# Windowed-attention block of a transformer kernel: shifted input and rotary tables made in earlier stages, query norms applied as the scale of the exponential, one wait moved

## The reference, cut to what matters

```python
h = shift_token(x)                    # channels 64..127 come from the token before
q, k, v = split(h @ wqkv)             # 8 heads of 64
q = l2norm(q) * qs;  k = l2norm(k) * ksc
q, k = rotary_xpos(q, k)              # q*cos*scale + rotate_half(q)*sin*scale, k with 1/scale
o = local_attention(q*8, k, v)        # windows of 64 tokens, 128 keys each, masked softmax
x = x + o @ wo
h = layernorm(shift_token(x)) * lg + lb
a, g = split(h @ w1 + b1);  x = x + (a * gelu(g)) @ w2 + b2
```

## Time and profile before

| | us |
|---|---|
| median of 3 runs | 1410.14 |
| the 3 runs | 1409.4 to 1416.5 |
| the profiled execution | 1428.19 |
| its span (first to last instruction) | 1426.4 |
| PE busy | 1167.5 (82%) |
| DVE busy | 915.8 (64%) |
| ACT busy | 588.9 (41%) |
| POOL busy | 420.4 (29%) |

### The profile page before, as it was taken

The page is one execution under the profiler, slowest core; times in us unless marked ns, Lnnn a source line. Parts: engine busy times, 40 slices in busy tenths (PEclk is TensorE's granted clock), DMA queues, the critical chain, the costliest instruction groups (busy, mean ns, idle before and its releaser), DMA issues. The chain is left out here.

```text
span 1426.4 us, 28851 instructions
## 1 busy us (share of the span) xinstructions
PE 1167.5 (82%) x11197; PEld 708.9 (50%) x11197; DVE 915.8 (64%) x1538; ACT 588.9 (41%) x1379; POOL 420.4 (29%) x357
## 2 busy tenths in 40 slices
PE   7899887899797768897867989556996799963997
PEld 5477644687544347652436754323662354422343
DVE  3677544777346867534885724487465689979387
ACT  2555434555333549533557822200562255420100
POOL 0366301566003875300884500433341000000000
PEclk9899999899987989999997999889997899975699
DMA  2000000000021210011220001000000011110011
GB/s 58 15 1 2 1 12 17 1 1 1 9 71 41 56 34 3 2 61 24 57 50 2 3 6 66 12 3 4 4 5 12 12 20 19 19 34 0 8 29 44
DMA packets 55146, 29.29 MB, mean 21 GB/s; under 512 B 37634, under 2 KB 48620, under 8 KB 54508
## 3 DMA queue, kind: packets, MB, share of 16 engines
q1 hardware_dynamic: 55020, 27.52, 7.8%
HBM read 18.32 MB, written 1.06 MB: 14 GB/s over the span
## 5 line engine op out<-in xcount | busy, mean ns | idle before, releaser
L287 POOL TENSOR_TENSOR A_pr<-A_pr,A_rs 128x1024 f32<-128x1024 f32 x64 | 121.1, 1893 | 78.4 <-DVE A_rs L350 76.1
L340 DVE TENSOR_REDUCE A_mx<-psb 128x1 f32<-128x1024 f32 x64 | 77.8, 1216 | 15.2 <-PE psb L300 14.8
L1058 POOL TENSOR_TENSOR F_raw<-F_raw,F_rc 128x1024 f32<-128x1024 f32 x32 | 75.3, 2354 | 39.8 <-DVE F_raw L1133 39.8
L1077 PE MATMUL psb<-F_wqkv,F_hst 128*128 128x512 f32 x128 | 66.0, 640 | 16.6 <-ACT F_hst L1149 16.6
L383 ACT ACTIVATE A_pr<-psb,A_nm 128x1024 f32<-128x1024 f32 x64 | 71.2, 1112 | 20.1 <-DVE A_nm L344 20.1
L321 PE MATMUL psb<-A_pt,A_V 128*64 128x128 f32 x1024 | 63.0, 275 | 13.8 <-issue 8.9
L1943 PE MATMUL psb<-M_hb,M_wd 128*128 128x512 f32 x128 | 73.3, 657 | 0.0
L1088 PE MATMUL psb<-ident,F_raw 128*128 128x128 f32 x256 | 38.5, 298 | 42.2 <-POOL F_raw L1061 42.2
L1750 ACT ACTIVATE M_hall<-psb,M_bu 128x512 f32<-128x512 f32 x64 | 44.0, 687 | 64.8 <-PE psb L1701 64.8
L310 PE MATMUL psb<-ident,A_pr 128*128 128x128 f32 x512 | 68.8, 278 | 1.4 <-ACT A_pt L390 1.4
L1701 PE MATMUL psb<-XL,M_wu 128*128 128x512 f32 x128 | 68.7, 619 | 1.5 <-ACT M_ST L1761 1.1
(11 more groups left out here) (331 smaller groups left out, 2979.4 us busy)
## 6 DMA issues: line engine op xcount, KB each, us to landing
F_VS<-F_V SPq DMA_DIRECT2D x62, 128.0 KB, 2.3
F_raw<-in_c_xpos_dram SPq DMA_DIRECT2D x3, 1024.0 KB, 4.8
F_wqkv<-in_L_ffn_wqkv_dram SPq DMA_DIRECT2D x3, 768.0 KB, 6.2
A_w<-in_L_attn_w_dram SPq DMA_DIRECT2D x4, 256.0 KB, 3.0
M_wu<-in_L_ffn_Wup_dram SPq DMA_DIRECT2D x16, 64.0 KB, 2.0
M_wg<-in_L_ffn_Wgate_dram SPq DMA_DIRECT2D x16, 64.0 KB, 2.1
M_wd<-in_L_ffn_Wdown_dram SPq DMA_DIRECT2D x16, 64.0 KB, 1.8
M_sel<-in_c_select_dram SPq DMA_DIRECT2D x16, 64.0 KB, 1.9
```

The lines of the kernel that those rows point to most:

```text
L287: pool.tensor_tensor(p, p, rs[:, u % 2:u % 2 + 1].broadcast_to([P, SEQ]), ALU.mult).then_inc(scaled, 1)
L340: dve.tensor_reduce(mx[:, u % 2:u % 2 + 1], sview(u), AX, ALU.max).then_inc(maxed, 1)
L1058: pool.tensor_tensor(rs[:, o, :], rs[:, o, :], rc[:, o, :], ALU.add).then_inc(unit, 1)
L1077: pe.matmul(bank[2 * o + i], hst[:, o, :], wqkv[:, i * HD:(i + 1) * HD], start=True, stop=True)
```

## The change

Seven edits. The shifted copy of `H` is made in `XL` chunk by chunk in n3 and at the end of F4 (`shift_lower` on POOL, `shift_upper` on ACT) in place of F1. The rotary tables are made by POOL in A4 and in F4 (`rope_tables`) in place of DVE in F1, and their sources are loaded in A2 and F4. In F1 POOL multiplies only the keys by their inverse norms (512 columns for 1024) and copies the 8 inverse query norms of the tile to a new tile `F_RQ`. In F2 the exponential takes that norm as its scale, a per-partition column in place of the constant 8, and DVE's negated maximum is multiplied by it too (the 8 goes into the tables). In `rope`, the wait for the transposes of tile n-2 stands ahead of the three multiplications and no longer ahead of the sum of squares. In norms with `add` (n3 and n5), PE runs six matmuls of 128 columns into an unused bank before its first real one.

```diff
+        def layer_norm(tag, src, dst, gain=None, bias=None, loads=None, shift=False, add=None, shifted=None):
...
+                        if add is not None:
+                            for i in range(6):
+                                pe.matmul(psb[:, 7, 0:P], centre[:], ident[:], start=True, stop=True)
...
+                        if shifted is not None:
+                            for c in range(NCH):
+                                act.wait_ge(scaled, c + 1)
+                                shift_upper(act, dst, shifted, c)
+
+                    if shifted is not None:
+                        @block.gpsimd
+                        def _(pool):
+                            for c in range(NCH):
+                                pool.wait_ge(scaled, c + 1)
+                                shift_lower(pool, dst, shifted, c)
 
                     @block.vector
                     def _(dve):
...
+                        if shifted is not None:
+                            dve.memset(shifted[P // 2:P, :].rearrange("p (b n) -> p b n", b=NB)[:, :, 0:1], 0.0)
...
+                    @block.sync
+                    def _(sp):
+                        sp.wait_ge(loaded, loads(sp, loaded))
...
+        def window_attention(tag, Q, K, V, VS, RQ, masks, prs, pt):
...
+                def norms(n):
+                    t, j = first_token(n) // P, groups[n][2]
+                    return RQ[:, t:t + HW // 2, 2 * j:2 * j + 2].rearrange("p k h -> p h k")
...
-                            dve.tensor_scalar(nm[:, n % 2, :], mx[:, n % 2, :], -scale, None, ALU.mult).then_inc(negated, 1)
+                            dve.scalar_tensor_tensor(out=nm[:, n % 2, :].rearrange("p (h k) -> p h k", h=2), in0=mx[:, n % 2, :].rearrange("p (h k) -> p h k", h=2),
+                                                     scalar=-1.0, in1=norms(n), op0=ALU.mult, op1=ALU.mult).then_inc(negated, 1)
...
-                                last = act.activation(prs[n % NP][:, w, :], sview(n)[:, w, :], ACT.Exp, bias=nm[:, n % 2, w:w + 1], scale=scale,
+                                last = act.activation(prs[n % NP][:, w, :], sview(n)[:, w, :], ACT.Exp, bias=nm[:, n % 2, w:w + 1],
+                                                      scale=RQ[:, first_token(n) // P + w % 4, 2 * groups[n][2] + w // 4:2 * groups[n][2] + w // 4 + 1],
...
+        def rope_tables(pool, sem):
+
+
+
+            for i in range(2):
+                r = raw[:, i, :, :].rearrange("p s (t d) -> p s t d", d=FD)
+                f = tab[:, i, :, :].rearrange("p s (t d) -> p s t d", d=FD)
+                s = qks[:, i, :]
+                pool.tensor_tensor(f[:, 0], r[:, 0], s.unsqueeze(1).broadcast_to([P, TPS, FD]), ALU.mult)
+                for lo, hi in ((0, 32), (32, 0)):
+                    last = pool.tensor_tensor(f[:, 1, :, lo:lo + 32], r[:, 1, :, lo:lo + 32],
+                                              s[:, hi:hi + 32].unsqueeze(1).broadcast_to([P, TPS, 32]), ALU.mult)
+            last.then_inc(sem, 1)
+
+        def shift_lower(pool, src, dst, c):
+            pool.tensor_copy(dst[0:P // 2, cs(c)], src[0:P // 2, cs(c)])
+
+        def shift_upper(act, src, dst, c):
+            o = c * CH + (1 if c * CH % SEQ == 0 else 0)
+            act.activation(dst[P // 2:P, o:(c + 1) * CH], src[P // 2:P, o - 1:(c + 1) * CH - 1], ACT.Copy)
+
...
-                    full_attention("A2", QS, KH, KL, V3, DH ** -0.5, att, bv[:, 0:1])
+                    full_attention("A2", QS, KH, KL, V3, DH ** -0.5, att, bv[:, 0:1],
+                                   lambda sp, sem: issue(sp, sem, table_parts(0) + window_weights(0) + [
+                                       (mask[:].bitcast(U16), a["c_window"].rearrange("p (v n) -> p v n", v=2))]))
...
+                        rope_tables(pool, tabled)
...
+            layer_norm("n3", X, H, add=H, shifted=XL)
...
+                    RQ = sb("F_RQ", [P, NT, HEADS], stack=sa)
...
-                                pool.wait_ge(unit, 2 * n + 1)
+                                pool.wait_ge(unit, 3 * n + 1)
                                 pool.wait_ge(inv, n + 1)
-                                pool.tensor_tensor(rs[:, o, :].rearrange("p (h d) -> p h d", d=DH), rs[:, o, :].rearrange("p (h d) -> p h d", d=DH),
-                                                   rn[:, o, :].unsqueeze(2).broadcast_to([P, 2 * HEADS, DH]), ALU.mult).then_inc(unit, 1)
+                                k = rs[:, o, HD:2 * HD].rearrange("p (h d) -> p h d", d=DH)
+                                pool.tensor_tensor(k, k, rn[:, o, HEADS:2 * HEADS].unsqueeze(2).broadcast_to([P, HEADS, DH]), ALU.mult).then_inc(unit, 1)
+                                pool.tensor_copy(RQ[:, ds(n, 1), :].rearrange("p o h -> p (o h)"), rn[:, o, 0:HEADS]).then_inc(unit, 1)
                             finish(0, 0, True)
...
-                                pe.wait_ge(unit, 2 * n + 2)
+                                pe.wait_ge(unit, 3 * n + 2)
...
-                            dve.memset(hs[HALF:P, :].rearrange("p (b n) -> p b n", b=NB)[:, :, 0:1], 0.0).then_inc(moved, 1)
-                            dve.tensor_copy(hs[0:HALF, :], H[0:HALF, :]).then_inc(moved, 1)
...
-                            last.then_inc(scaled, 1)
-                            dve.wait_ge(scaled, 1)
-
                             def rope(n, o, first):
                                 dve.wait_ge(squared, n + 1)
                                 if not first:
-                                    dve.wait_ge(turned, n - 1)
+                                    dve.wait_ge(unit, 3 * n - 3)
                                 t = n % TPS
...
-                                step(dve.tensor_reduce(rn[:, o, :], sq[:, o, :].rearrange("p (h d) -> p h d", d=DH), AX, ALU.add))
-                                dve.tensor_scalar(rn[:, o, :], rn[:, o, :], 1e-24, None, ALU.max).then_inc(summed, 1)
+                                step(dve.tensor_reduce(norms, sq[:, o, :].rearrange("p (h d) -> p h d", d=DH), AX, ALU.add))
+                                dve.tensor_scalar(norms, norms, 1e-24, None, ALU.max).then_inc(summed, 1)
+                                if not first:
+                                    dve.wait_ge(turned, n - 1)
                                 dve.tensor_tensor(c3, src, factor(0, 0, DH), ALU.mult)
...
-                                dve.reciprocal(rn[:, o, :], rn[:, o, :]).then_inc(inv, 1)
+                                dve.reciprocal(norms, norms).then_inc(inv, 1)
...
-                            v = H[HALF:P, :].rearrange("p (b n) -> p b n", b=NB)
-                            w = hs[HALF:P, :].rearrange("p (b n) -> p b n", b=NB)
-                            act.activation(w[:, :, 1:SEQ], v[:, :, 0:SEQ - 1], ACT.Copy).then_inc(moved, 1)
...
-                            act.wait_ge(moved, 3)
...
+                        issue(sp, drawn, table_parts((l + 1) % LAYERS))
+                        sp.wait_ge(loaded, issue(sp, loaded, window_weights((l + 1) % LAYERS)))
+
+                    @block.gpsimd
+                    def _(pool):
+                        pool.wait_ge(drawn, 16 * 3)
+                        rope_tables(pool, tabled)
+                        pool.wait_ge(tabled, 1)
+                        for c in range(NCH):
+                            pool.wait_ge(added, c + 1)
+                            shift_lower(pool, H, XL, c)
...
+                            if u > NJ and u % NJ == 2:
+                                act.wait_ge(added, u // NJ)
+                                shift_upper(act, H, XL, u // NJ - 1)
+                        act.wait_ge(added, NCH)
+                        shift_upper(act, H, XL, NCH - 1)
...
+                            if c % 2 == 0:
+                                dve.memset(XL[P // 2:P, c * CH:c * CH + 1], 0.0)
...
-    tabs = [np.cos(fr) * sc, np.sin(fr) * sc * sgn, np.cos(fr) / sc, np.sin(fr) / sc * sgn]
+    tabs = [np.cos(fr) * sc * 8, np.sin(fr) * sc * sgn * 8, np.cos(fr) / sc, np.sin(fr) / sc * sgn]
```

More of the change, by code:

```diff
@@ L125, in build @@
             clear([loaded, turned, kept, made])
-        def layer_norm(tag, src, dst, gain=None, bias=None, loads=None, shift=False, add=None):
+        def layer_norm(tag, src, dst, gain=None, bias=None, loads=None, shift=False, add=None, shifted=None):
             g = loaded, moved, centred, squared, held, var_rdy, std_rdy, inv, spread, scaled, normed = sems(
@@ L255, in project_add, with full_attention @@
             clear(g)
-        def full_attention(tag, Q, KH, KL, V, scale, result, bias):
+        def full_attention(tag, Q, KH, KL, V, scale, result, bias, loads):
             KB = SEQ // P
@@ L263, in full_attention @@
             NP = 4
-            g = (scored, maxed, negated, exped, inverted, scaled, turned, kept_a, kept_v, mixed, put_out) = sems(
-                "full", "scored maxed negated exped inverted scaled turned kept_a kept_v mixed put_out")
```

(46 more changed lines are left out.)

80 lines of the change are left out of this document (30 added, 50 removed).

## The result

| | before | changed |
|---|---|---|
| median of the runs | 1410.37 us (4 runs) | 1436.51 us (4 runs) |
| lowest and highest | 1409.4 and 1416.5 | 1426.05 and 1447.51 |
| the profiled execution | 1428.19 | 1426.05 |
| its span | 1426.4 | 1424.3 |

The changed kernel is slower: the ratio of the runs is 1.0133, 95% interval 1.0077 to 1.0190, which on 1410.4 us is 1429. The ratio leaves out one of the four runs (1447.51), in which the core ran at a lower clock; the plain median of 1436.51 has it in, and the median of the other three is 1434.1.

The account below looks back on a forecast made before the run. No engine bounds the whole: ACT bounds F2; POOL's add, then DVE's three products, set F1's period. Terms 20.6 - 1.8 - 3.8 + 2.1 - 7.2 = +9.9 us on 1410.1 gave 1420, range 1403 to 1430.

Parts of the forecast that it names:

- the two loops: F2's period was to rise from 3.32 to 4.01 us, and F1's was to stay at 4.78 us.
- the first rival: In n3 the six matmuls gain nothing; +7.2 and their 0.7 us cost remain, giving 1428 us; chance 0.17.
- Exponentials, +20.6: In F2 a second pointer operand costs 0.086 us an exponential, 0.69 a group, over both layers +20.6 us.
- Fewer columns and the moved wait, -1.8: In F1 the period stays 4.78 us; only the last tile's shorter POOL multiplication shows, 0.9 us a layer, twice.
- F1's front, -3.8, and ends, +2.1: ACT's shift of 1904 ns leaves F1's start twice; copies after the last chunk add 0.7 us three times (n3, F4 twice).
- Six matmuls ahead of n3, -7.2: n3 regains the upper clock by less PE idling: 7.95 us gained less 0.7 for a later first real matmul.
- From the profile to the runs: The sum +9.9 puts the profiled execution at 1438 us; the same sum on 1410.1 gives 1420.
- The rival with F1's period at 1397: F1's period falls because POOL's total or DVE's own time was the bound: 1397 us, faster; chance 0.08.

## Why the prediction was half right

The prediction was slower, 1420 us, 1403 to 1430. The sign and the two loops are right; the size is not. The plain median of 1436.5 is above the range, and the 1429 of the ratio is at its upper end, where the first rival stood with 1428. That the ratio lies inside the range is owed to this rival, which was given 0.17, and not to the sum of the forecast.

- *Exponentials, +20.6*: right in F2. The profile gives 19.8, the seven profiles with the pointer and the seven without 21. The runs give 23, and what the sum had at nothing is the clock: lower stretches late in F2 and at the start of F4, which only kernels with the pointer show, about 1.5 and 2 us. The pointer's price was 0.094 for the 0.086 taken, and 0.09 a group was won back. The Trainium skill's 93 ns (ScalarE: Activation LUTs, What ACT_TABLE_LOAD costs) is the better price, and the trace agrees with it.
- *Fewer columns and the moved wait, -1.8*: right, 0.9 a layer and a period of 4.79 both times. The reason given was right as to the place (the clip waits for POOL's add) and too narrow as to the cause: it is not the `tensor_scalar` alone, the `tensor_tensor` between SBUF tiles is held as well.
- *F1's front, -3.8, and ends, +2.1*: right, within what the clock blurs. F1 of layer 0 is 2.3 us shorter for 2.8, F4 of layer 1 0.68 longer for 0.7, and layer 0's F4 with layer 1's F1 comes to -1.9 for -2.1 once the slow start of that F4 is taken off: VectorE's second product there starts 5.48 us behind the stage's first matmul (631.08 less 625.60) for 3.78 before (632.28 less 628.50), 1.7 us.
- *Six matmuls ahead of n3, -7.2*: **this step failed.** The prediction took n3's clock of 0.59 in one execution for a property of the code ("n3 missed it by little"). In the profiles it varies, 0.60, 0.88 and 1.00, with the same instructions ahead. The term is worth nothing that the runs can tell, 1.0026 alone and 1.0128 for 1.0144. Without its gain, and with the 0.7 that it costs, the sum is the first rival's, 17.8 us or 1428. In the two profiles the term came out at -7.4 (12.52 us from the first add to the last scaling, 426.19 less 413.67, for 19.89), and this made the 11.4 look like the 9.9. That is luck: the execution before had drawn the low clock.
- *From the profile to the runs*: the sum was made against an execution that lay 18 us above its median, and the prediction said that the waits in it were no clock effects but for n3's. That exception was the point: it was carried over to runs that need not share it.
- The rival with F1's period at 1397 was given 0.08 and needed a clip that isn't held. It is what happens once the clip is freed, by 10 us a layer.

What stays open: why the clock falls in n3 in one execution and not in another, whether the six matmuls prevent the longest of these falls, and by what mechanism the slower F2 brings low stretches late in it and at the start of F4.

## What to carry to other kernels

Moving work off an engine pays only in the loop that holds the period: here POOL lost half of a multiplication and VectorE a wait, and both went into the hold of one 16-column instruction. An instruction that is much longer than its columns, and always ends with another engine's, names the real bound; freeing it (one input from PSUM, or none at all) was worth 20 us on the changed kernel, as much as the whole change had cost. Operands are not free: a per-partition scale in place of a constant costs a fixed price per instruction, here 0.094 us on a spacing of 0.342, and what they cost can show in the next stage too. And before a stretch at low clock goes into a sum, look for the same stretch in a second execution, of any kernel that has the same code up to there.
